# Norms, gates and transposes of four tiles at a time, and ScalarE's queue re-ordered, in a convolution, attention and LoRA kernel on one Trainium2 core

## The reference

```
x = x + layernorm(attn(layernorm(x)))
x = x + layernorm(ffn(layernorm(x)))
```

## Time and profile before

| what | value |
|---|---|
| median of 3 runs | 945.75 us (943.86 to 947.29) |
| the profiled execution's own time | 943.72 us |
| its span, first to last instruction | 941.9 us |
| mean granted TensorE clock | 0.916 of full speed |
| busy: PE, its weight loads, DVE, ACT, POOL | 764.8, 680.6, 617.8, 388.8, 332.7 us |

### The profile page before, as it was taken

The page is one execution under the profiler, slowest core; times in us unless marked ns, Lnnn a source line. Parts: engine busy times, 40 slices in busy tenths (PEclk is TensorE's granted clock), DMA queues, the critical chain, the costliest instruction groups (busy, mean ns, idle before and its releaser), DMA issues.

```text
span 941.9 us, 14710 instructions
## 1 busy us (share of the span) xinstructions
PE 764.8 (81%) x5136; PEld 680.6 (72%) x5136; DVE 617.8 (66%) x1794; ACT 388.8 (41%) x964; POOL 332.7 (35%) x316
## 2 busy tenths in 40 slices
PE   2579856999967986999967985999967988997471
PEld 1578845788867974888957974888867986786371
DVE  6999934897573475887573574797573473565936
ACT  3443434776323234675214234666223334552122
POOL 2565562566424311455323321456223311221000
PEclk9989977999998998999988997999987999999656
DMA  7257884342965574312935574322845574223002
GB/s 224 79 204 243 278 288 145 112 149 98 311 209 186 187 265 179 116 64 88 324 119 197 179 275 161 102 78 68 318 141 179 167 247 157 79 91 112 0 1 89
DMA packets 104058, 153.31 MB, mean 163 GB/s; under 512 B 7344, under 2 KB 75952, under 8 KB 103984
## 3 DMA queue, kind: packets, MB, share of 16 engines
q1 hardware_dynamic: 93744, 120.90, 38.7%
q10 hardware_dynamic: 10240, 31.46, 8.8%
HBM read 120.88 MB, written 31.46 MB: 162 GB/s over the span
## 4 chain that ended last, share of the span: by engine, by line
PE 42%; DVE 33%; issue 8%; DMA 6%; ACT 5%; POOL 3%; SPq 2%; ACTq 0%; DVEq 0%; POOLq 0%
PE bank L751 9%; PE bank L752 8%; PE bank L753 8%; PE bank L847 4%; PE bank L828 4%; PE bank L885 3%; PE bank L836 2%; DVE work L1325 2%; DVE v L1248 2%; DVE stats L1316 2%; POOL k_t L1383 2%; DVE stats L1250 2%; DVE work L1257 2%; DVE ln_r L1096 2%; DMA out<-work 2%
## 5 line engine op out<-in xcount | busy, mean ns | idle before, releaser
L751 PE MATMUL bank<-f_hi,w_pair 128*128 128x256 f32 x768 | 229.9, 299 | 59.5 <-POOL w_pair L1376 38.9
L752 PE MATMUL bank<-f_lo,w_pair 128*128 128x256 f32 x768 | 223.4, 291 | 0.0
L753 PE MATMUL bank<-f_hi,w_pair 128*128 128x256 f32 x768 | 223.2, 291 | 0.0
L1376 POOL TENSOR_TENSOR w_pair<-raw,w_pair 128x512 fp32r<-128x512 f32 (+1 forms) x111 | 143.4, 1303 | 204.6 <-ACT w_pair L951 204.4
L751 PEld LDWEIGHTS bank<-f_hi,w_pair 128*128 128x128 f32 x768 | 153.5, 200 | 65.8 <-issue 25.4
L752 PEld LDWEIGHTS bank<-f_lo,w_pair 128*128 128x128 f32 x768 | 154.1, 201 | 0.5
L753 PEld LDWEIGHTS bank<-f_hi,w_pair 128*128 128x128 f32 x768 | 153.5, 200 | 0.0
L1387 POOL TENSOR_TENSOR prob<-prob,rtotal 128x512 f32<-128x512 f32 x64 | 84.4, 1331 | 193.4 <-DVE rtotal L1221 193.4
L1001 ACT ACTIVATE prob<-prob,ntop 128x128 f32<-128x128 f32 x256 | 99.3, 391 | 46.9 <-DVE ntop L1217 46.8
L951 ACT ACTIVATE w_pair<-raw 128x512 fp32r<-128x512 f32 (+1 forms) x120 | 71.0, 610 | 78.7 <-PE bank L753 52.7
L1383 POOL TENSOR_TENSOR k_t<-q_t 128x256 f32<-128x256 f32 x48 | 37.8, 808 | 80.3 <-ACT q_t L968 75.0
(11 more groups left out here) (130 smaller groups left out, 1633.3 us busy)
## 6 DMA issues: line engine op xcount, KB each, us to landing
w_pair<-kept_pairs SPq DMA_DIRECT2D x120, 512.0 KB, 4.4
raw<-conv_w SPq DMA_DIRECT2D x96, 256.0 KB, 4.2
kept_pairs<-w_pair ACTq DMA_DIRECT2D x40, 512.0 KB, 3.6
work<-x SPq DMA_DIRECT2D x32, 512.0 KB, 7.0
out<-work ACTq DMA_DIRECT2D x16, 512.0 KB, 4.5
w_pair<-kept_pairs SPq DMA_DIRECT2D x24, 256.0 KB, 3.0
v<-conv_w SPq DMA_DIRECT2D x12, 256.0 KB, 3.3
kept_pairs<-w_pair ACTq DMA_DIRECT2D x8, 256.0 KB, 2.7
```

The costliest lines, as they stand in the source:

```text
L751: pe.matmul(dst, w_h, m_h, start=start, stop=False)
L752: pe.matmul(dst, w_h, m_l, start=False, stop=False)
L753: return pe.matmul(dst, w_l, m_h, start=False, stop=stop)
L1376: pool.tensor_tensor(lo, raw_of(k)[:, 0:n], hi.bitcast(F32), ALU.subtract).then_inc(*split_low_pool.now(k))
```

## The change

Norm two, norm three, the gates and the transposes of their result take `n` tiles instead of always two; in batches 0 to 2 n is four. Norm three's scaling by ACT is put 13 ticks after slot 11, at slot 24. The output projection alternates four banks. Chunks that are not convolution weights get a lead of 2 in place of 5, and no split behind such a chunk is put before it. The x tiles 2 and 3 of the next batch are loaded, and the statistics of tiles 0 and 1 taken, among the first v projections, and norm one's `std` and `scale_x` stand behind the softmax of the first pair of heads. `mid2` and `mid_t` now lie in `o_lo` and `o_hi`.

```
-LEAD, KEEP_LEAD = 5, 2
-NORM3_LAG, OUT_LAG, STORE_LAG = 1, 4, 1
+LEAD, SLOW_LEAD, KEEP_LEAD = 5, 2, 2
+OUT_LAG, STORE_LAG = 4, 1
 SIDE = [
-    (9, "project_out"), (10, "add_norm2", 0), (12, "add_norm2", 2), (14, "norm3", 0), (18, "norm3", 2),
-    (24, "lora_turn", 0), (25, "lora_mid", 0), (26, "lora_turn", 1), (27, "lora_mid", 1), (29, "gates", 0),
-    (30, "lora_turn", 2), (31, "lora_mid", 2), (32, "lora_turn", 3), (33, "lora_mid", 3), (35, "turn_mid", 0),
-    (35, "gates", 2), (36, "lora_out", 0), (41, "turn_mid", 2), (42, "lora_out", 2),
-    (44, "next_x", 0), (44, "next_x", 1), (47, "next_x", 2), (47, "next_x", 3), (47, "next_stats", 0), (47, "next_stats", 1),
+    (9, "project_out", ("side", "turn") * 2), (10, "add_norm2", 0, TB), (11, "norm3", 0, TB, 12),
+    (25, "lora_turn", 0), (26, "lora_mid", 0), (27, "lora_turn", 1), (28, "lora_mid", 1), (29, "lora_turn", 2),
+    (30, "lora_mid", 2), (31, "lora_turn", 3), (32, "lora_mid", 3), (33, "gates", 0, TB), (36, "turn_mid", 0, TB),
+    (37, "lora_out", 0, 2), (42, "lora_out", 2, 2), (45, "next_x", 0), (45, "next_x", 1),
 ]
 TAIL = [
-    ("project_out", ("side", "side", "stream", "stream")), ("add_norm2", 0), ("tick",), ("norm3", 0, 1), ("add_norm2", 2), ("tick",),
-    ("norm3", 2, 1), ("lora_turn", 0), ("lora_mid", 0), ("tick",), ("lora_turn", 1), ("lora_mid", 1), ("tick",), ("gates", 0),
-    ("lora_turn", 2), ("lora_mid", 2), ("lora_turn", 3), ("lora_mid", 3), ("tick",), ("turn_mid", 0), ("gates", 2),
-    ("lora_out", 0, ("side", "v")), ("turn_mid", 2), ("lora_out", 2, ("stream", "turn")),
+    ("project_out", ("side", "side", "stream", "stream")), ("add_norm2", 0, 2), ("tick",), ("norm3", 0, 2, 1), ("tick",),
+    ("add_norm2", 2, 2), ("tick",), ("norm3", 2, 2, 1), ("lora_turn", 0), ("lora_mid", 0), ("tick",), ("lora_turn", 1),
+    ("lora_mid", 1), ("tick",), ("gates", 0, 2), ("lora_turn", 2), ("lora_mid", 2), ("tick",), ("lora_turn", 3), ("lora_mid", 3),
+    ("tick",), ("turn_mid", 0, 2), ("gates", 2, 2), ("lora_out", 0, 2, ("side", "v")), ("turn_mid", 2, 2),
+    ("lora_out", 2, 2, ("stream", "turn")),
 ]
...
+    def ahead(self, k):
+        upto = k
+        while upto + 1 < len(CHUNKS) and upto < k + (LEAD if CHUNKS[upto + 1][0] == "conv" else SLOW_LEAD):
+            upto += 1
+        return upto
     def use_chunk(self, *name, over=True):
         k = NUMBER[name]
-        self.split_chunks(k + LEAD)
+        self.split_chunks(self.ahead(k))
...
-    def norm3(self, b, t0, lag=NORM3_LAG):
-        self.put("x1_stats", b, t0)
-        self.std("ln3", b, t0, PR)
-        self.later(lag, lambda: self.put("scale3", b, t0))
+    def norm3(self, b, t0, n, lag):
+        self.later(1, lambda: self.put("x1_stats", b, t0, n))
+        self.later(1, lambda: self.std("ln3", b, t0, n))
+        self.later(1 + lag, lambda: self.put("scale3", b, t0, n))
...
             for t in range(TB):
                 self.tick()
                 self.project_v(b, 0, t)
+                if more and t >= 2:
+                    put("load_x", b + 1, t)
+                    put("x_stats", b + 1, t - 2)
...
                     put("normalise", b, i - 1, 1)
+                    if i == 1 and more:
+                        self.std("ln1", b + 1, 0, TB)
+                        for t in range(TB):
+                            put("scale_x", b + 1, t)
...
                 if i == 0 and more:
                     for t in (TB - 2, TB - 1):
                         put("x_stats", b + 1, t)
-                    self.std("ln1", b + 1, 0, TB)
-                    for t in range(TB):
-                        put("scale_x", b + 1, t)
...
-        mid2 = sb("mid2", [P, PR, 2 * ER], F32R)
-        mid_t = sb("mid_t", [P, PR, P], F32R)
+        mid2, mid_t = (tile[:, :].rearrange("p (t n) -> p t n", t=TB) for tile in (o_lo, o_hi))
```

More of the change, by code:

```diff
@@ L78, in side @@
     for s, stage, *args in SIDE:
-        if b < 0 and stage not in ("next_x", "next_stats"):
+        if b < 0 and stage != "next_x":
             continue
@@ L324, in lora_mid, with gates, turn_mid, lora_out @@
         self.later(1, lambda: self.put("mid_out", b, t))
[L326 to L334, removed]
+    def gates(self, b, t0, n):
+        self.put("gates", b, t0, n)
+    def turn_mid(self, b, t0, n):
+        self.take(("turn_mid", b, t0), "turn", "mid_t", b, t0, n)
+        self.put("turn_mid", b, t0, n)
+    def lora_out(self, b, t0, n, kinds=("side", "turn")):
+        for t, kind in zip(range(t0, t0 + n), kinds):
             for j in range(2):
                 self.take(("lora_out", b, t, j), kind, "ln4", b, t, j)
-        self.put("lora_out", b, t0)
-        self.std("ln4", b, t0, PR)
+        self.put("lora_out", b, t0, n)
+        self.std("ln4", b, t0, n)
         def scale():
-            self.put("out_scale", b, t0)
-            self.later(STORE_LAG, lambda: self.put("store", b, t0))
+            self.put("out_scale", b, t0, n)
+            self.later(STORE_LAG, lambda: self.put("store", b, t0, n))
         self.later(OUT_LAG, scale)
@@ L600, in back @@
             return divmod(b * size + i - by, size)
-        pairs = lambda name: [(b, t) for b, t0 in at(name) for t in (t0, t0 + 1)]
+        tiles = lambda name: [(b, t) for b, t0, n in at(name) for t in range(t0, t0 + n)]
         tiles_by_half = lambda name: [(b, t, half) for b, t in at(name) for half in range(2)]
@@ L617, in build @@
         mid_turned = Signal(sem("mid_turned"), at("turn_mid"))
-        delta = Signal(sem("delta"), [(b, t, j) for b, t in pairs("lora_out") for j in range(2)])
+        delta = Signal(sem("delta"), [(b, t, j) for b, t in tiles("lora_out") for j in range(2)])
         x_scaled_act = Signal(sem("x_scaled_act"), [s for s in at("scale_x") if s[1] < TB // 2])
@@ L666, in build @@
         attn_out = Signal(sem("attn_out"), at("proj_bias"))
[L667 removed]
+        x1_done = Signal(sem("x1_done"), tiles("add_norm2"))
         logits_out = Signal(sem("logits_out"), at("mid_out"))
@@ L671, in build @@
         mid2_full = Signal(sem("mid2_full"), at("gates"))
-        ln4_added = Signal(sem("ln4_added"), [(b, t, j) for b, t in pairs("out_scale") for j in range(2)])
+        ln4_added = Signal(sem("ln4_added"), [(b, t, j) for b, t in tiles("out_scale") for j in range(2)])
         lora_low = Signal(sem("lora_low"), [(i,) for i in range(2)])
@@ L720, in build @@
         c_turn = lambda c: C_ORDER.index(c)
+        mid_ready = lambda b, t: next(mid_t_full(*s) for s in at("turn_mid") if s[0] == b and s[1] <= t < s[1] + s[2])
         def bank_free(kind, *event):
@@ L1286, in link @@
                     step[0] += 1
-                for t in range(t0, t0 + PR):
+                for t in range(t0, t0 + n):
                     w.wait_ge(*logits_out(b, t))
-                link(dve.tensor_reduce(gtop[:, :], logits[:, :, :], AX.X, ALU.max))
-                dve.tensor_tensor(gexp[:, :, :], logits[:, :, :], spread(gtop, E), ALU.subtract).then_inc(*shifted.now(b, t0))
-                dve.tensor_tensor(above[:, :, :, :], other, own, ALU.is_gt)
-                link(dve.tensor_tensor(tied[:, :, :, :], other, own, ALU.is_equal))
@@ L1294, in gates @@
-                link(dve.tensor_tensor(tied[:, :, :, :], tied[:, :, :, :], before[:, :, :, :], ALU.mult))
-                link(dve.tensor_tensor(above[:, :, :, :], above[:, :, :, :], tied[:, :, :, :], ALU.add))
-                link(dve.tensor_reduce(rank[:, :, :], above[:, :, :, :], AX.X, ALU.add))
-                w.wait_ge(*gexp_done(b, t0))
-                link(dve.scalar_tensor_tensor(out=gate[:, :, :], in0=rank[:, :, :], scalar=float(TOP_K), in1=gexp[:, :, :],
+                link(dve.tensor_reduce(gtop[:, ts], logits[:, ts, :], AX.X, ALU.max))
@@ new lines, in gates @@
+                dve.tensor_tensor(gexp[:, ts, :], logits[:, ts, :], spread(gtop, E), ALU.subtract).then_inc(*shifted.now(b, t0, n))
+                dve.tensor_tensor(above[:, ts, :, :], other, own, ALU.is_gt)
+                link(dve.tensor_tensor(tied[:, ts, :, :], other, own, ALU.is_equal))
+                link(dve.tensor_tensor(tied[:, ts, :, :], tied[:, ts, :, :], before[:, ts, :, :], ALU.mult))
+                link(dve.tensor_tensor(above[:, ts, :, :], above[:, ts, :, :], tied[:, ts, :, :], ALU.add))
@@ L1313, in lora_out @@
+                link(dve.tensor_copy(mid2[:, ts, 0:ER], mid[:, ts, :]))
+                dve.tensor_tensor(mid2[:, ts, ER:2 * ER], mid[:, ts, :], mid2[:, ts, 0:ER].bitcast(F32),
+                                  ALU.subtract).then_inc(*mid2_full.now(b, t0, n))
+            def lora_out(b, t0, n):
+                for t in range(t0, t0 + n):
                     for j in range(2):
```

143 lines of the change are left out of this document (69 added, 74 removed).

## The result

| | kernel before | changed kernel |
|---|---|---|
| median | 945.12 us (4 runs) | 932.18 us (4 runs, 929.38 to 934.71) |
| ratio to before | | 0.986, interval 0.9825 to 0.9895 |
| the profiled execution, its span | 943.72, 941.9 us | 934.71, 932.9 us |
| granted clock | 0.916 | 0.922 |

The kernel got faster by 12.9 us, 1.4%, where 37 were forecast, and 932 lies above the whole range of 892 to 925. A second set of runs of the changed kernel gave 933.54 us, 0.9861 (0.9828 to 0.9894).

The account below looks back on a forecast made before the run. PE was taken to wait on a chain of DVE's norms, ACT's scaling and split, and POOL's subtraction. Terms summed to -37.0 us: 906.7 profiled, 908.7 as median, rounded to 908; range 892 to 925.

Parts of the forecast that it names:

- ScalarE's lead, batch 0: Value projections of batch 0: with lead 2, two blocked splits come behind the copies of v, so PE goes on sooner; -9 us.
- the same lead at the end of batch 0's attention: Output projection, batch 0: splits come behind `finish_wo` and `conv_out`, and POOL hardly outruns PE's passes; +1.4 us.
- Nothing new is late: Rival, chance 0.15: all of the convolution slots' loss but 3.1 us goes, attention in batches 1 and 2 starts as before; 886 us.
- DVE's queue takes the place of ACT's: Rival, chance 0.17: POOL's splits and sums lengthen DVE's block, PE waits about 10 us at slot 24; 924 us.
- Slower: Rival, chance 0.03: late loads of the residual x hold DVE, `conv_split` and the splits behind one DMA; some 954 us.
- the fourth rival: Chance 0.02: `conv_split` holds ACT as long as the scaling did, start of attention takes the other gains; no change, 945 us.
- The norms: Norms two and three, slots 10 to 24, batches 0 to 2: later scaling stops ACT's standstill, one DVE block; -24.4 us together.
- The DMA wait of 3.1: Convolution slots of batch 0: PE's DMA wait stays and shortens the wait at slot 24 by as much; 3.1 us.
- The rule that the Trainium skill states: DVE operations with two SBUF inputs and GpSimd operations reading SBUF exclude each other throughout; one-input statistics are spared.
- LoRA slots: Gates and transposes of four tiles: the transpose at slot 41 goes with its waits; -1.7 us each, -5 together.
- Start of attention, batches 1 and 2: Norm one behind the first softmax delays `turn_x`, and x tile 3 loads later; +2.5 us each, +5 together.
- Tail: End of the kernel: tiles 2 and 3 no longer scaled ahead of ACT's copies of tile 1, last `mid_out` sooner; -5 us.

## Why the prediction was wrong

**The step that failed is "ScalarE's lead, batch 0"**, -9, together with its heads (nothing) and "the same lead at the end of batch 0's attention", +1.4. Measured: +4.8, +12.6 and +7.9, together 32.9 us worse. The splits were priced as they moved relative to `conv_out`, the copies of v and PE. What was not looked at is the other stage tied to these chunks, `keep`. Its lead of 2 was named in the diff as unchanged, and in the kernel before it was harmless: between a split five chunks ahead and a save two chunks ahead lie three uses, in which POOL is long done. With both at 2 the distance is nil. Also +1.4 came from comparing POOL's 1.29 us with PE's pass, as if ACT split freely; ACT's cycle for a kept chunk is 0.63 and 1.9 us of wait. "Nothing new is late", "DVE's queue takes the place of ACT's" and "Slower" all had the lead at -9, and the fourth rival had no sum, so the range could not hold the result. With the save taken out of the way the kernel runs in 909.02 us, and the first scores gain the most of what was forecast (-7.6). That 909 is near the 908 (the sum gave 908.7) is luck: at slot 10 it stands at +1.3 instead of -7.6, the norms gain more than forecast, and the two cancel. What takes the 8.9 us in the heads of that kernel was not tried.

**The norms.** The mechanism was right: one gap at slot 24, ended by POOL (4.59; forecast 5.1), ACT's long wait by `conv_add` (12.10), the block 1.9 longer by POOL's passes (2.2). The DMA wait of 3.1 that batch 0 was to keep did not come: its one gap is 4.58, and its 24.5 us are those of batches 1 and 2. The term was mis-sized: -24.4, measured -35.3. I held a remaining loss of 7.0 against a lost 15.0 counted for fifteen slots, but slot 24 itself begins at 505.57, so 36.2 us (from slot 10 at 469.33) hold fourteen slots: 16.6 lost. And the 0.9 for slow matmuls and 1.0 for `lora_turn` come after slot 24, where the kernel before pays for its own 5.10 us wait in the same way (0.55 for its first matmul too). The wait of 5.1 alone against 16.6 would have given 11.5 a batch; measured 11.7 to 11.9. The argument left the cause of the gain to the four-tile block and the late scaling together; the runs show that up to slot 24 it is the scaling.

**The rule that the Trainium skill states**, SBUF — State Buffer, Who interferes with whom, was weighed at 2.2 us of lengthening, and at 5.5 if every split met an addition. Measured: 1.9, with both sides lengthened, which agrees with its exclusive lock: the pass that began at 493.38, within the first addition (to 494.58), ended at 495.74, and the second addition, recorded from 494.50, ended at 496.82, each 1.1 to 1.2 us after the other's end. Of the exemption for one input little shows: two statistics beside the pass that began at 499.06 took 0.68 and 0.67, as alone (0.69). The argument that "the statistics showed no lengthening" had nothing under it, since POOL ran no pass beside them in the kernel before.

**The rest.** LoRA slots: -5 forecast, -8.1 measured. Start of attention, batches 1 and 2: +5, measured +8.0, and its cause was not the one forecast. 4.9 of it (2.7 and 2.2) are there by the first scores, ahead of norm one's new place, as the 4.3 of batch 3 are. Putting norm one first took only 1.9 off these two stretches in the changed kernel and 3.0 with the lead of five; putting the loads back took nothing off the time. The value projections of batch 3, +4.3, were not in the sum: I had looked for the price of the next input there, and it arises without one. What it comes from stays open. Tail: -5, measured -4.8 to the last `lora_mid` in the first profile and -8.9 in the second, where the clock had risen.

## What to carry to other kernels

When a stage is moved in an in-order queue, list every stage that names the same buffer or chunk and compare their distances after the move: a wait that was free three uses behind its producer costs the full round trip over the other engine directly behind it. A save that needs another engine's result belongs late, or on a queue that carries no critical work (the second was not tried here). And before merging tiles to shorten a block, try to move only the instruction that blocks the queue: here that was two numbers in a list, worth 21 us of 945.

## What was unexpected of the hardware

The same tail at two clocks. In one execution of the changed kernel PE had 0.50 for 20 us and in another 0.90 and 1.00 after the same first 5; the tail differs by 4.2 us of 933. In the kernel before, the corresponding matmuls ran at 3.68 us for 16 in the profiled execution, the slow level. So one profile against one profile can be 4 us off in the tail alone, as much as a part of this change is worth; to say which kernel is faster, the medians of four runs are used.
